# Eight array tiles for windowed attention: both sequences' scores and values together, seven shared PSUM banks, one set of rotary DMAs per pair

## The reference

```python
q, k, v = split(x @ Wqkv)                      # 16 heads of 64
q = l2norm(q) * qs;  k = l2norm(k) * ksc
q = q * cos * scale + rotate_half(q) * sin * scale
k = k * cos / scale + rotate_half(k) * sin / scale
# windows of 32 queries, each sees its own 32 keys and the 32 before
sim = einsum('bhwie,bhwje->bhwij', bq, bk2) * 8.0
attn = softmax(where(mask, -max, sim))
x = x + einsum('bhwij,bhwje->bhwie', attn, bv2) @ Wo
x = x + (a * gelu(gate)) @ W2 + b2             # (a, gate) = layernorm(x) @ W1 + b1
```

## Time and profile before

| | us |
|---|---|
| median of 3 runs | 3714.94 (3714.89 to 3717.26) |
| the profiled execution | 3724.61 |
| its span in the profile | 3722.6 |
| PE busy | 3402.5 (91%) |
| DVE busy | 3223.6 (87%) |
| ACT busy | 2227.8 (60%) |
| POOL busy | 2052.1 (55%) |
| mean granted clock | 0.96 |

### The profile page before, as it was taken

The page is one execution under the profiler, slowest core; times in us unless marked ns, Lnnn a source line. Parts: engine busy times, 40 slices in busy tenths (PEclk is TensorE's granted clock), DMA queues, the critical chain, the costliest instruction groups (busy, mean ns, idle before and its releaser), DMA issues.

```text
span 3722.6 us, 144192 instructions
## 1 busy us (share of the span) xinstructions
PE 3402.5 (91%) x62248; PEld 1871.9 (50%) x62248; DVE 3223.6 (87%) x5344; ACT 2227.8 (60%) x3808; POOL 2052.1 (55%) x1787
## 2 busy tenths in 40 slices
PE   6899999999999999985676799999999999999996
PEld 2455555555555555542333355555555555555553
DVE  5899999999999999874776799999999999999984
ACT  3566576665666666652453466666766667666663
POOL 3666566555666656642433565665656656565552
PEclk8999999999999999996877999999999999999998
DMA  4232332232332322200001332232232332332320
GB/s 126 68 79 70 75 81 73 72 81 70 80 77 70 85 70 72 73 17 12 0 0 54 78 76 73 70 87 69 73 85 67 78 83 67 77 82 66 77 49 24
DMA packets 200483, 250.08 MB, mean 67 GB/s; under 512 B 52012, under 2 KB 95656, under 8 KB 199848
## 3 DMA queue, kind: packets, MB, share of 16 engines
q1 hardware_dynamic: 199848, 240.86, 25.9%
HBM read 36.18 MB, written 3.15 MB: 11 GB/s over the span
## 4 chain that ended last, share of the span: by engine, by line
PE 30%; DVE 12%; issue 4%; ACT 3%; POOL 1%; DMA 1%; SPq 0%; POOLq 0%; DVEq 0%; ACTq 0%
PE general L566 4%; PE attp L580 4%; PE general L628 3%; PE scores L598 3%; PE sums L608 2%; PE general L636 2%; PE general L645 2%; PE general L638 1%; PE proj_k L554 1%; DVE k_ring L1232 1%; DVE sines L752 1%; DVE q_ring L758 1%; DVE probs_t L845 1%; PE proj_q L554 1%; PE proj_q L556 1%
## 5 line engine op out<-in xcount | busy, mean ns | idle before, releaser
L1107 POOL TENSOR_TENSOR k_ring<-k_ring,partner 128x512 f32<-128x512 f32 x384 | 499.0, 1299 | 362.1 <-DMA partner<-sines 359.9
L1116 POOL TENSOR_TENSOR probs<-probs,q_scale 128x512 f32<-128x512 f32 x384 | 401.8, 1046 | 396.8 <-DVE probs L828 396.8
L1122 POOL TENSOR_TENSOR probs<-probs,row_sum 128x512 f32<-128x512 f32 x384 | 407.8, 1062 | 358.3 <-DVE row_sum L839 358.2
L1107 POOL TENSOR_TENSOR q_ring<-q_ring,partner 128x512 f32<-128x512 f32 x384 | 491.2, 1279 | 50.4 <-DMA partner<-sines 50.4
L954 ACT ACTIVATE squares<-proj_q 128x512 f32<-128x512 f32 x384 | 229.0, 596 | 402.4 <-PE proj_q L556 401.0
L580 PEld LDWEIGHTS attp<-probs_t,v_buf 32*64 32x64 f32 x24576 | 393.0, 133 | 147.4 <-issue 141.8
L566 PE MATMUL general<-att,wo 128*128 128x512 f32 x768 | 376.2, 624 | 74.0 <-ACT att L1013 74.0
L580 PE MATMUL attp<-probs_t,v_buf 32*64 32x64 f32 (+1 forms) x24576 | 435.5, 218 | 5.1 <-ACT att L1013 5.1
L752 DVE SCALAR_TENSOR_TENSOR sines<-proj_q,vec,consts 128x512 f32<-128x512 f32 x384 | 278.7, 726 | 170.1 <-ACT squares L954 149.7
L628 PE MATMUL general<-wv,xs 128*32 128x256 f32 x6144 | 413.2, 387 | 3.1 <-DVE rstd L727 1.7
L598 PE MATMUL scores<-k_ring,q_ring 64*32 64x64 f32 (+1 forms) x24576 | 405.0, 215 | 0.0
(11 more groups left out here) (149 smaller groups left out, 6835.5 us busy)
## 6 DMA issues: line engine op xcount, KB each, us to landing
partner<-sines SPq DMA_DIRECT2D x3072, 64.0 KB
wqk_raw<-in_wqkv SPq DMA_DIRECT2D x80, 128.0 KB
wv<-in_wqkv SPq DMA_DIRECT2D x12, 512.0 KB, 4.4
wo<-in_wo SPq DMA_DIRECT2D x12, 512.0 KB, 4.7
w<-in_w SPq DMA_DIRECT2D x12, 341.0 KB, 3.3
base_dram<-x SPq DMA_DIRECT2D x8, 256.0 KB, 2.7
att<-in_wqkv SPq DMA_DIRECT2D x4, 512.0 KB, 5.8
q_ring<-base_dram SPq DMA_DIRECT2D x8, 256.0 KB, 3.1
```

What stands on the lines that cost most here:

```text
L1107: e.tensor_tensor(y, y, partner[:, which, :], ALU.add).then_inc(S[f"rotated_{side}"], 1)
L1116: e.tensor_tensor(y, y, spread_keys(scale), ALU.mult).then_inc(S["q_norms_off"], 1)
L1122: e.tensor_tensor(y, y, spread_keys(row_sum[:, b, :]), ALU.mult).then_inc(S["probs_done"], 1)
```

## The change

- Scores and values now work on one group (four heads) of both sequences at a time, on even steps alone: 64 matmuls instead of 32, `q ^ seq` choosing the head so that the second sequence takes the four tiles that the first leaves free. v and the k norms' spread are laid out to match (`q ^ seq` in `pe_v`, `spread_sel` twice as large, so the spread has four matmuls of half the width).
- Scores are issued in two halves (windows 0 to 3, 4 to 7) with sums, the projection of q and the spread between them. The two halves of the values stand one behind the other, but for an `enter` stage in the first items.
- DVE's, POOL's and ACT's stages on the probabilities take 1024 columns instead of 512, half as often. The subtraction of the maximum is on DVE, before as after; it now comes last in the step. `probs` holds two groups instead of three halves.
- The copy of k's inverse norms out of PSUM goes from DVE to ACT (`act_k_inv`).
- Seven of the eight banks form one ring that `Banks` hands out in program order, also to projections, scores and values; the banks of the scan keep a fixed place.
- `sines` has two buffers; q and k of a pair move together in four DMAs of 128 KB, once both are written and both additions of the pair before are done.
- The ring of rotated q and k has 11 slots instead of 12. Values, exponents and turns lag one step more, v one less. The three gates of the feed-forward are made in one step, its values in the next two. The order within each engine's step is another.

```diff
-RING = 12
+RING = 11
+POOL_BANKS = 7
...
-EXP_LAG = SCORES_LAG + 1
-TURN_LAG = SCORES_LAG + 2
-VALUES_LAG = SCORES_LAG + 3
-V_LAG = 5
-PROBS = 3
+OFF_LAG = SCORES_LAG + 1
+EXP_LAG = SCORES_LAG + 2
+TURN_LAG = SCORES_LAG + 3
+VALUES_LAG = SCORES_LAG + 4
+V_LAG = 4
+PROBS = 2
...
+    def group(self, t, lag):
+        n, p = divmod(t - lag, SUBSTEPS)
+        return (n, p // 2) if p % 2 == 0 and 0 <= n < ITEMS else None
...
     def use(self, key, sem, value):
-        self.of[key] = len(self.uses)
-        self.uses.append((sem, value))
+        at = self.next
+        self.next = (at + 1) % self.banks
+        self.of[key], self.before[key] = at, self.last.get(at)
+        self.last[at] = (sem, value)
...
+            for win in windows:
+                for seq in range(CHUNK_SEQS):
+                    for q in range(4):
+                        h = q ^ seq
+                        slot, r0 = slot_of(n, 2 * group + h // 2), DH * (h % 2)
+                        t0, back = seq * SEQ + win * WIN, WIN if win else 0
+                        qw = qk_ring[0][r0:r0 + DH, slot, t0:t0 + WIN]
+                        kw = qk_ring[1][r0:r0 + DH, slot, t0 - back:t0 + WIN]
+                        o = g[seq][32 * q:32 * q + 32, win * 2 * WIN + WIN - back:(win + 1) * 2 * WIN]
+                        done = e.matmul(o, qw, kw, start=False, stop=True, skip_group_check=True)
...
+            for kb in blocks:
+                for seq in range(CHUNK_SEQS):
+                    for q in range(4):
+                        h = q ^ seq
+                        o = g[2 * seq + h // 2][DH * (h % 2):DH * (h % 2) + DH, kb * WIN:kb * WIN + width]
+                        done = e.matmul(o, lhs, rhs, start=(kb == 0), stop=True, skip_group_check=True)
...
+        def move_partners(e, w, k, n, p):
+            i = (k * ITEMS + n) * PAIRS + p
+            w.wait_ge(S["sin_q"], i + 1)
+            w.wait_ge(S["sin_k"], i + 1)
+            w.wait_ge(S["rotated_q"], i)
+            w.wait_ge(S["rotated_k"], i)
+            for r in range(0, P, WIN):
+                to = r + WIN if r % DH == 0 else r - WIN
+                e.dma_start(partner[to:to + WIN, :, :], sines[r:r + WIN, i % 2, :, :]).then_inc(S["moved"], 16)
...
+        def act_k_inv(e, w, k, n, group):
+            i = (k * ITEMS + n) * GROUPS + group
+            w.wait_ge(S["norm_spread"], i + 1)
+            w.wait_ge(S["k_norms_off"], 2 * i)
+            e.activation(k_inv[:, WIN:], general_of(("spread", k, n, group))[:, :], ACT.Copy).then_inc(S["k_inv_kept"], 1)
```

More of the change, by code:

```diff
@@ L109, in __init__ @@
         self.root = self.item(t, 24)
-        self.hidden = next(((self.item(t, 25 + j), j) for j in range(len(HIDDEN_CUTS)) if self.item(t, 25 + j) is not None), None)
+        self.gates = self.item(t, 25)
+        self.values_of = next(((self.item(t, at), js) for at, js in ((26, (0,)), (27, (1, 2))) if self.item(t, at) is not None), None)
         self.ffn_out = self.item(t, 28)
@@ L186, in stack @@
             g = k * ITEMS
+            if st.scores:
+                n, group = st.scores
+                for seq in range(CHUNK_SEQS):
+                    self.use(("scores", k, n, group, seq), "k_norms_off", ((g + n) * GROUPS + group) * 2 + seq + 1)
+            if st.var is not None:
+                self.var(("ffn", k, st.var))
+            if st.out_last is not None:
+                self.use(("project", k, st.out_last, 2), "att_added", (g + st.out_last) * 3 + 3)
+            if st.now:
+                n, p = st.now
+                self.use(("proj", k, n, p, 0), "cos_q", (g + n) * PAIRS + p + 1)
             if st.spread:
@@ L335, in macaron_kernel @@
         out_tiles = out.rearrange("b (h p) d -> p (b h) d", p=P)
-        tiles = [qk_ring[k][:, i, :] for k in (0, 1) for i in range(RING)]
+        tiles = [qk_ring[k][:, i, :] for k in (0, 1) for i in range(RING)] + [att[:, i, :] for i in range(2)]
         m_xn, m_z, m_e, m_ln, m_corr, m_y = tiles[0:6]
@@ L824, in dve_sub @@
-        def dve_sub(e, w, k, n, s):
-            i, b = (k * ITEMS + n) * SUBSTEPS + s, s % 2
+            for seq in range(CHUNK_SEQS):
+                start = k_inv[:, seq * SEQ:seq * SEQ + 1]
+                keys = bass.AP(start.tensor, start.offset, [list(start.ap[0]), [WIN, NWIN], [1, 2 * WIN]])
+                y = probs[:, i % PROBS, seq * COLS:(seq + 1) * COLS]
+                e.tensor_tensor(cube(y), cube(general_of(("scores", k, n, group, seq))[:, :]), keys, ALU.mult).then_inc(S["k_norms_off"], 1)
@@ L1424, in constants @@
     for head in range(HEADS):
-        c[norm_row(head // 2, 1) + head % 2, C_SPREAD + head * WIN:C_SPREAD + (head + 1) * WIN] = 1
+        for seq in range(CHUNK_SEQS):
+            at = C_SPREAD + seq * GROUPS * P + (head ^ seq) * WIN
+            c[norm_row(head // 2, 1) + head % 2, at:at + WIN] = 1
     return c
```

463 lines of the change are left out of this document (241 added, 222 removed).

## The result

The changed kernel takes 3747.6 us (median of 7 runs), the kernel before 3717.3 us in runs beside it: ratio 1.0071, 95% interval 1.0054 to 1.0089. It is slower by 0.7%, where 3476 us and 6.4% faster had been forecast.

The account below looks back on a forecast made before the run. PE bounds first, DVE 4.6 us per item behind. Pitch 66.58 to 61.5 over 44 intervals saves 224 us, starts and tails cost 15 of gain more: 3724.6 - 239 = 3486, adjusted by 9.7 to 3476 us; range 3360 to 3715.

Parts of the forecast that it names:

- PE's scores and values: PE's two attention stages: eight tiles side by side, 1.16 us instead of 1.96 and 1.06 instead of 2.12.
- The slower rival: PE's scores and values: eight tiles start no denser than four, pitch 68.1 us, 3782 us; chance 13%.
- DVE's work: DVE's load per item: falls from 62.0 to 58.4 us by the k_inv move, fewer reciprocals and fewer start-ups.
- the walk of meetings: PE and DVE meeting four times an item, fixed loads between: round closes at 61.0 us, 61.5 taken.
- the bank ring: Seven shared banks in fixed order: PE's values wait for DVE's scaling of the scores, 1.2 us for both banks.
- orders cost more: ACT's queue comes late for squares or k_inv: pitch about 64 us, half of the gain, 3586 us; chance 18%.
- k_inv: Copy moved from DVE to ACT, four an item: 2.3 us off DVE, ACT no busier than before.
- The clock: PE's granted clock: the forecast is wrong if it falls below 1.00 in the stacks; no size given.
- No loss in moving both halves together: Partner DMAs of q and k moved together: no loss seen with sines held twice, no steady-state gain.
- The range's upper end: Whole kernel's time: 3715 us, leaving out the slower case; some 19% outside the range.
- the case of nothing gained: PE gains half of the eight tiles and the meetings take it back: pitch 66.6 us; chance 5%.
- fourth case: In the forecast's odds, the only case within 0.2% (7.4 us) of no change: 5%.

Follow-up runs that it names:

- e7_plight: Changed kernel without the second half of the scores (64 of 128 records of each pair of sequences left out): ratio 1.0038 to the kernel before.
- e12_banks: Changed kernel with each use taking the one of the seven banks that comes free first, instead of the ring: ratio 1.0031 to the kernel before.
- e18_before_kinv: Kernel before the change with only the k_inv copy moved from DVE to ACT: ratio 1.0069 to the kernel before.
- e11_fill: Changed kernel with six idle matmuls in front of the second group's values of each item: ratio 1.0044 to the kernel before.
- e15_moves: Changed kernel with partner DMAs in two sets of four, and POOL adding q, then k, then the entry: ratio 1.0046 to the kernel before.
- e9_orders: Changed kernel with the same instructions reordered on PE, DVE, ACT and POOL, and some lags one step later: ratio 0.9767 to the kernel before.
- e10_orders_four: The kernel of e9_orders with four tiles for both sequences (h = q): ratio 0.9759 to the kernel before.
- e19_kinv_dve: Changed kernel with k_inv copied by DVE again, right in front of its scaling of the scores: ratio 1.0427 to the kernel before.
- e14_few: Changed kernel with a few order moves on PE, DVE and POOL, both halves of the scores together: ratio 1.0185 to the kernel before.
- e6_dlight: Changed kernel with DVE's subtraction of the maximum on one of sixteen windows only: ratio 0.9956 to the kernel before.

## Why the forecast was wrong

- **PE's scores and values** were taken at 7.7 ns a record with a small charge for each half. They cost 12 per record at the stage: 1.52 and 1.50 us instead of 1.16 and 1.06. The first 32 records of a burst start 8 ns apart; behind them comes a stop, and the second 32 average 12. The saving was 3.9 us per item in the two stages where 7.4 had been taken; that eight tiles run side by side was right. The slower rival, that they start no denser than four, is refuted though its sign came true.
- **DVE's work** was right: 58.9 us per item for 58.4.
- **The step that failed is the walk of meetings**, 61.0 closed and 61.5 taken. At that pitch DVE, with 58.4 us of work, would stand 3.1 us per item; it stands 6.7 with 58.9, and the two together are the distance from 61.5 to the 65.6 of the sample. For PE the walk added 2.7 us of waiting to the 1.6 that the pitch of the kernel before already holds, 4.3; measured are 5.3, and PE's work is 60.3 where 57.2 had been taken (65.0 less 7.8). This mis-sized work is not what sets the pitch, since in e7_plight 3.2 us off PE brought only 0.3%. Who waits for whom came as forecast, DVE for the squares and PE for the scaling; how long did not. The walk gave the bank ring as the cause; taking the ring's wait away (e12_banks) brought 0.4%. It treated each engine's stretch as fixed and looked for the later of two. The runs fit a loop through projection, square, rotation, scaling, values and back, though none follows it link by link: 3.2 us off PE gave 0.3%, 4.9 us off DVE 1.1%, shorter squares 1.1%, other orders 3.0%. Other orders return 2.0 of the 4.9 us per item between 61.5 and the 66.3 of all intervals; the other 2.9 stay open. The rival "orders cost more" (18%) named this, with ACT's queue and k_inv in it, and e18_before_kinv shows that head-of-line wait by itself; it was priced at half the gain instead of all.
- **The clock** was a condition for being wrong and had no price. What PE saved became waits, and half clock behind them, 4.2 us per item for 0.4. It is a small part of the loss: e11_fill took 2.3 us of it away for 0.2 us of time.
- **"No loss in moving both halves together"** looked at the steady stretch alone, where it holds. At the starts it cost most of 23 us in the trace (19 came back in e15_moves), nearly the 25.5 us by which the traces differ, though the time of e15_moves fell by 0.25% only, which its interval does not tell from nothing.
- **k_inv** was taken as 2.3 us gained in a queue with room. Room in ACT's total is not room in front of the squares.
- The range's upper end, 3715, was the time of no change. The slower side was given a single mechanism and 13%, and a sum of several small ones, starts, clock and meetings, was not in it.
- Two slips in the rivals: by the formula of the forecast the case of nothing gained gives 3700, not 3715, and is the third and not the fourth case; and the slower case leaves out the 15 us at the starts and tails. Neither moves the range.

Open: what bounds e9_orders and e10_orders_four at the same 64.5 us with DVE 92 to 93% busy; how much of the 3.5% of e19_kinv_dve is the copy and how much its place; why values wait for "issue" after 128 scores in a row; and how much of the 1.0 us of pitch that the first stack gains and the second does not is chance between executions.

## What to carry to other kernels

In a kernel whose two busiest engines hand work to each other several times per step, price an edit by what the meeting engines wait for next: here a microsecond off one engine was worth 0.2 at most, one more on DVE ahead of its scaling cost a whole one (k_inv), and the same instructions in another order were worth 2 us an item. Change the orders of the queues first and the work second, and judge a part of a change in the order that it will run in (k_inv on ACT: 0.7% slower in one, 3.5% faster in the other). Look at the ramps by themselves: a merge of transfers that is free in the steady state can hold up a start.

## What the runs showed of the hardware

- Eight tiles start records of 32 to 64 columns 8 ns apart for the first 32; then come two steps of 39 and 47 ns, and the second 32 average 12. With 128 in a row the average is 10.2 (e14_few) to 10.5. Pieces of 32 keep the 8 ns (0.24 us a piece) and lose it in the switches (0.37 from start to start).
- A wait of 1.75 us on PE was followed by 6.9 us at 1.2 GHz, in which v took 1.9 times as long; idle matmuls in the wait took away half of such stretches (4.2 to 1.9 us per item) and brought 0.3%.
- POOL's multiplication of probabilities by their sums took 2.76 us for 1024 columns where two of 512 took 2.13 before. It runs beside DVE's subtraction for 1.0 us of that. With 15/16 of the subtraction left out (e6_dlight) it took 1.90. The Trainium skill ("GPSIMD Engine Reference", section "Specifications") has POOL share its SBUF interfaces with DVE's instructions of two SBUF inputs, of which the subtraction is one; these rows agree. So e6 took some 3.4 us per item off POOL as well as 4.9 off DVE, and its 1.1% is the price of both.

```profile
L1198 POOL TENSOR_TENSOR probs<-probs,row_sum 128x1024 f32<-128x1024 f32 x65 | 179.3, 2759 | 158.8 <-DVE row_sum L907 158.7
```

```profile
L1199 POOL TENSOR_TENSOR probs<-probs,row_sum 128x1024 f32<-128x1024 f32 x66 | 125.7, 1904 | 164.4 <-DVE row_sum L908 164.4
```
